# Attention: a chunk's value sum turned by TensorE transposes into unused score columns, its parts added by GpSimd

## The reference

```python
qkv = x @ w_attn
...
att = jnp.einsum('bhtd,bhsd->bhts', q, k) * (1.0 / math.sqrt(hd))
causal = jnp.tril(jnp.ones((T, T), dtype=bool))
att = jnp.where(causal, att, -jnp.inf)
att = jax.nn.softmax(att, axis=-1)
...
att = att.reshape(B, H, 2, T, T)
att = att[:, :, 0] - lambda_full * att[:, :, 1]
out = jnp.einsum('bhts,bhsd->bhtd', att, v)
```

## Time and profile before

| | us |
|---|---|
| median of 3 executions | 3572.49 (3572.16 to 3578.31) |
| the profiled execution | 3580.86 |
| its span | 3579.1 |
| PE busy in it | 3336.4 (93%) |
| DVE busy | 2745.6 (77%) |
| ACT busy | 2214.7 (62%) |
| POOL busy | 1518.2 (42%) |

### The profile page before, as it was taken

One profiled execution on the slowest core, in us unless ns is written; L12 is line 12 of the kernel. 1 busy time (PEld: TensorE's weight loads), 2 busy tenths in 40 slices (PEclk: granted clock), 3 DMA queues, 4 the chain that ended last, 5 costly groups with the idle time before them and its releaser, 6 DMA issues. The chain is left out here.

```text
span 3579.1 us, 59642 instructions
## 1 busy us (share of the span) xinstructions
PE 3336.4 (93%) x19650; PEld 1381.1 (39%) x19663; DVE 2745.6 (77%) x4938; ACT 2214.7 (62%) x3459; POOL 1518.2 (42%) x1881
## 2 busy tenths in 40 slices
PE   8998999999999999999999999866999999999997
PEld 5564666643333333333333333252333333333332
DVE  4654223568898888898898889384899989899898
ACT  3331221137777777777777777745777767777763
POOL 2225000013333332323333333313887888887886
PEclk9999999989999999999999999987999999999999
DMA  4443111111111111110111110041222222222221
GB/s 154 132 156 110 45 44 44 42 35 40 49 38 31 35 37 34 33 32 26 29 34 34 34 31 25 11 136 53 61 82 75 69 80 74 69 80 75 66 75 53
DMA packets 160886, 211.60 MB, mean 59 GB/s; under 512 B 32324, under 2 KB 108364, under 8 KB 160604
## 3 DMA queue, kind: packets, MB, share of 16 engines
q1 hardware_dynamic: 141340, 172.51, 16.3%
q0 software_dynamic: 8512, 18.76, 1.7%
q10 hardware_dynamic: 10752, 16.78, 1.4%
HBM read 154.48 MB, written 52.69 MB: 58 GB/s over the span
## 5 line engine op out<-in xcount | busy, mean ns | idle before, releaser
L1270 ACT ACTIVATE prob<-psS 128x1024 f32<-128x1024 f32 (+3 forms) x1280 | 1100.2, 905 | 332.0 <-PE psS L1437 326.1
L1329 DVE TENSOR_REDUCE pmax<-psR 128x1 f32<-128x512 f32 x1674 | 1060.8, 684 | 139.2 <-PE psR L1384 100.1
L1384 PE MATMUL psR<-kslab,qslab 48*128 48x512 bf16 (+3 forms) x2480 | 675.2, 353 | 55.6 <-DVE pmax L1329 23.0
L2100 POOL TENSOR_TENSOR hc<-h_d,crep 128x512 f32<-128x512 f32 x512 | 647.2, 1272 | 184.2 <-DVE h_d L2318 135.9
L1437 PE MATMUL psS<-qslab,kslab 51*128 51x512 bf16 (+3 forms) x2560 | 638.0, 351 | 5.1 <-ACT prob L1270 4.4
L1452 PE MATMUL psVo<-prob,vaug 128*32 128x512 f32 (+3 forms) x5120 | 625.2, 544 | 0.9 <-ACT ov L1274 0.9
L1202 POOL TENSOR_SCALAR_AFFINE_SELECT prob<-prob 128x256 f32<-128x256 f32 (+1 forms) x512 | 209.3, 421 | 774.0 <-ACT prob L1270 773.7
L2318 DVE TENSOR_TENSOR_SCAN h_d<-a,state,psU 128x512 f32<-128x512 f32 x384 | 489.4, 1275 | 0.0
L1384 PEld LDWEIGHTS psR<-kslab,qslab 48*128 48x128 bf16 x2480 | 181.7, 94 | 789.7 <-DVE pmax L1329 462.1
L2308 DVE TENSOR_TENSOR psU<-dtx,psX 128x512 f32<-128x512 f32 x512 | 355.9, 695 | 119.5 <-PE psX L2471 44.3
L2225 ACT ACTIVATE a<-dt,a_neg 128x512 f32<-128x512 f32 x512 | 366.2, 723 | 57.8 <-DVE h_d L2318 56.5
(11 more groups left out here) (297 smaller groups left out, 4854.4 us busy)
## 6 DMA issues: line engine op xcount, KB each, us to landing
crep<-c_rows_d SPq DMA_DIRECT2D x256, 256.0 KB, 3.2
x_e<-rows_d SPq DMA_DIRECT2D x72, 128.0 KB, 2.0
y_d<-y SPq DMA_DIRECT2D x72, 128.0 KB, 1.7
q_d<-parts SPq DMA_DIRECT2D x48, 128.0 KB, 2.4
k_d<-parts SPq DMA_DIRECT2D x48, 128.0 KB, 4.1
qslab<-q_d SPq DMA_DIRECT2D x60, 96.0 KB
kslab<-k_d SPq DMA_DIRECT2D x60, 96.0 KB
x<-in_L_attn_x_dram SPq DMA_DIRECT2D x8, 512.0 KB, 5.9
```

Of the source, the lines that this page charges most:

```text
L1270: act.activation(prob[g % BUFS][:, :, off:BLK], psS[g % 2][:, :, off:BLK], ACT.Exp).then_inc(prob_ready, 1)
L1329: dve.tensor_reduce(into[:, lo:lo + (count - 1) * NEXT + 1:NEXT], psR[at % BANKS][:, 0:count * w].rearrange("p (n w) -> p n w", w=w), AX.X ...
L1384: ins = pe.matmul(dst[:, m * w:(m + 1) * w], qslab[u][rows, i * P:(i + 1) * P], kslab[u][rows, ch * BLK:ch * BLK + w], start=(m == 0), sto ...
L2100: pool.tensor_tensor(hc[:, g % CR], h[:, g % HR], crep[:, g // PAIR % SPR], ALU.mult).then_inc(hc_ready, 1)
```

## The change

Per chunk, `fold_sum` no longer takes a bank of `psR`. It turns the four blocks of `ov` with float32 transposes (`ident` as the moving operand, 128 columns each) into columns 0 to 255 of both banks of `psS[g % 2]`, on a diagonal step whose scores use columns 256 on only. The four folds stand at steps 11, 22, 38 and 50 (step 10 of the next head), after the step's lead item and ahead of its scores. ScalarE copies them after the step's exponentials, 4 x 4 x 17 columns, and the scores of step g+2 wait for that copy too. `o_head` now holds the even and the odd part apart. GpSimd adds them (`add_sums`, step 12 of the next head), VectorE takes the reciprocal there (step 14), and GpSimd multiplies by lambda and combines (step 16). The constant `fold` and what made it in the stage before go. The ring `psR` holds only max items and the turned maxima.

```diff
-        FOLD = LAG + 3
-        POST = FOLD + 3
...
+        FOLD_AT = [LAST[1], LAST[1] + TPB * 3 - 1, LAST[3] - 1, NSTEP + LAST[1] - 1]
+        for c, k in enumerate(FOLD_AT):
+            assert k > LAST[c] + LAG and STEPS[k % NSTEP][2] >= 2 * P
+        SUM_AT, WEIGHTS_AT, POST_AT = FOLD_AT[-1] + 2, FOLD_AT[-1] + 4, FOLD_AT[-1] + 6
+        END = TOTAL - NSTEP + POST_AT + 1
+        VALUES_AT = LAG + 3
...
-        o = sb("o_head", [P, 2, ST_T, 2, OC])
+        o = sb("o_head", [P, 2, ST_T, 2, 2, OC])
+        osum = sb("o_sum", [P, ST_T, 2, OC])
...
+            def add_sums(n):
+                pool.wait_ge(fold_copied, BPB * n + BPB + CREDIT)
+                pool.wait_ge(post, 5 * n + CREDIT)
+                pool.tensor_tensor(osum[:], o[:, n % 2, :, :, 0], o[:, n % 2, :, :, 1], ALU.add).then_inc(post, 1)
+
             def combine(n):
                 pool.wait_ge(rs_ready, n + 1 + CREDIT)
...
+                pool.wait_ge(post, 5 * n + 1 + CREDIT)
+                pool.tensor_tensor(rl[:], rs[:, :, 1], lam[:, 1:2].to_broadcast([P, ST_T]), ALU.mult).then_inc(post, 1)
...
-            def copy_fold(n, c):
-                at = PLACE[("fold", n, c)]
-                act.wait_ge(ring_full, at + 1 + CREDIT)
+            def copy_fold(g, n, c):
+                act.wait_ge(scores_done, min(g, TOTAL) + 1 + CREDIT)
                 if n >= 2:
-                    act.wait_ge(post_done, n - 1 + CREDIT)
-                act.copy(o[:, n % 2, TPB * c:TPB * c + TPB].rearrange("p i a d -> p (i a d)"),
-                         psR[at % BANKS][:, 0:TPB * 2 * OC]).then_inc(ring_free[at % BANKS], 1)
+                    act.wait_ge(post, 5 * (n - 1) + CREDIT)
+                act.copy(o[:, n % 2, TPB * c:TPB * c + TPB].rearrange("p (x y) a s d -> p x (y a s) d", x=2),
+                         psS[g % 2][:, :, 0:2 * P].rearrange("p x (y d) -> p x y d", d=VW)[:, :, :, 0:OC])\
+                   .then_inc(fold_copied, 1)
...
             def weights(n):
-                freed(dve, ("fold", n, BPB - 1))
-                dve.wait_ge(post_done, n + CREDIT)
-                dve.reciprocal(rs[:], o[:, n % 2, :, :, VD]).then_inc(rs_chain, 1)
-                dve.wait_ge(rs_chain, n + 1 + CREDIT)
-                dve.tensor_scalar(rl[:], rs[:, :, 1], lam[:, 1:2], None, ALU.mult).then_inc(rs_ready, 1)
+                dve.wait_ge(post, 5 * n + 1 + CREDIT)
+                dve.reciprocal(rs[:], osum[:, :, :, VD]).then_inc(rs_ready, 1)
...
+            def scores_free(g):
+
+                pe.wait_ge(prob_ready, min(g - 1, TOTAL) + CREDIT)
+                for m, c in folds_at(g - 2):
+                    pe.wait_ge(fold_copied, FOLDS.index((m, c)) + 1 + CREDIT)
+
+            def fold_sum(g, n, c):
+                scores_free(g)
                 pe.wait_ge(ov_ready, BPB * n + c + 1 + CREDIT)
-                dst = take(("fold", n, c))
                 for i in range(TPB):
-                    ins = pe.matmul(dst[:, i * 2 * OC:(i + 1) * 2 * OC], ov[c % 2][:, i * P:(i + 1) * P],
-                                    fold[:].rearrange("p a d -> p (a d)"), start=True, stop=True)
-                ins.then_inc(ring_full, 1)
+                    ins = pe.transpose(psS[g % 2][:, i // 2, i % 2 * P:i % 2 * P + P], ov[c % 2][:, i * P:(i + 1) * P],
+                                       keep["ident"][:])
+                if g >= TOTAL:
+                    ins.then_inc(scores_done, 1)
...
                 if lead:
                     max_products(lead[1], lead[2])
                     got = got[1:]
+                for n, c in folds_at(g):
+                    fold_sum(g, n, c)
                 if g < TOTAL:
                     scores(g, (1, 0) if lead and ITEMS[lead[2]][0] == 0 else (0, 1))
```

More of the change, by code:

```diff
@@ L651, in phase_experts @@
         kslabs, qslabs = keep["kslabs"], keep["qslabs"]
-        ident_b, mask_q, fold, lam_in, lam_s = (keep[x] for x in ("ident_b", "mask_q", "fold", "lam_in", "lam_s"))
+        ident_b, mask_q, lam_in, lam_s = (keep[x] for x in ("ident_b", "mask_q", "lam_in", "lam_s"))
         lam_w = sb("lam_w", [P, 2, HD])
@@ L780, in _ @@
             c.after(pool.memset(mask_q[:], 0.0))
-            c.after(pool.memset(fold[:], 0.0))
             c.after(pool.memset(keep["bias_d"][:], 0.0))
@@ L800, in _ @@
             c.wait()
-            for odd in range(2):
-                c.after(pool.affine_select(out=fold[:], in_=fold[:], compare_op=ALU.not_equal, fill=1.0,
-                                           base=-VW * odd, pattern=[[-2 * VW, 2], [-1, OC]], channel_multiplier=1))
         @block.scalar
@@ L978, in phase_attention @@
         LAG = 4
-        FOLD = LAG + 3
-        POST = FOLD + 3
         TURN = 2
         AHEAD = 0.26
-        END = TOTAL + POST + 1
         LAST = [max(k for k, s in enumerate(STEPS) if s[0] == c) for c in range(BPB)]
         DIAG = [k for k, (c, st, off, first) in enumerate(STEPS) if st >= TPB * c]
+        FOLD_AT = [LAST[1], LAST[1] + TPB * 3 - 1, LAST[3] - 1, NSTEP + LAST[1] - 1]
[4 more added lines that the diff above has]
+        VALUES_AT = LAG + 3
         MIX = 3
@@ L995, in phase_attention @@
         SLABS = 2
-        ident_b, mask_q, fold, lam_s = (keep[x] for x in ("ident_b", "mask_q", "fold", "lam_s"))
+        ident_b, mask_q, lam_s = (keep[x] for x in ("ident_b", "mask_q", "lam_s"))
         pmax = keep["pmax"]
@@ L1039, in phase_attention @@
         mpart_ready = sem("b_mpart_ready")
-        rs_chain = sem("b_rs_chain")
+        fold_copied = sem("b_fold_copied")
         rs_ready = sem("b_rs_ready")
-        pchain = sem("b_pchain")
+        post = sem("b_post")
         v_ready = sem("b_v_ready")
-        post_done = sem("b_post_done")
         mix_in = [sem(f"b_mix_in{s}") for s in range(MIX)]
@@ L1087, in fills_at, with folds_at @@
                 got.append(("turn", n + 1, 0))
[L1088 to L1091, removed]
-            return got
+            return got
+        def folds_at(g):
+            return [(m, c) for m in (g // NSTEP - 1, g // NSTEP) for c in range(BPB)
+                    if 0 <= m < NH and NSTEP * m + FOLD_AT[c] == g]
+        FOLDS = [fold for g in range(END) for fold in folds_at(g)]
         FILLS = [fills_at(g) for g in range(END)]
@@ L1203, in mask @@
                                    pattern=[[0, 2], [1, w]], channel_multiplier=-1).then_inc(prob_masked, 1)
+            def add_sums(n):
+                pool.wait_ge(fold_copied, BPB * n + BPB + CREDIT)
+                pool.wait_ge(post, 5 * n + CREDIT)
+                pool.tensor_tensor(osum[:], o[:, n % 2, :, :, 0], o[:, n % 2, :, :, 1], ALU.add).then_inc(post, 1)
             def combine(n):
                 pool.wait_ge(rs_ready, n + 1 + CREDIT)
[L1207 to L1213, removed]
+                pool.wait_ge(post, 5 * n + 1 + CREDIT)
+                pool.tensor_tensor(rl[:], rs[:, :, 1], lam[:, 1:2].to_broadcast([P, ST_T]), ALU.mult).then_inc(post, 1)
+                pool.tensor_tensor(o1[:], osum[:, :, 0, 0:VD], rs[:, :, 0:1].to_broadcast([P, ST_T, VD]), ALU.mult)\
+                    .then_inc(post, 1)
+                pool.wait_ge(post, 5 * n + 3 + CREDIT)
+                pool.tensor_tensor(o2[:], osum[:, :, 1, 0:VD], rl[:].unsqueeze(2).to_broadcast([P, ST_T, VD]),
+                                   ALU.mult).then_inc(post, 1)
+                pool.wait_ge(post, 5 * n + 4 + CREDIT)
+                pool.tensor_tensor(o_rows[:, n], o1[:], o2[:], ALU.subtract).then_inc(post, 1)
             def gather(n):
@@ L1247, in _ @@
                     mask(n, k)
-                if 1 <= n < NH - 1 and k == FOLD:
+                if 1 <= n < NH - 1 and k == VALUES_AT:
                     values(n + 1)
@@ L1255, in _ @@
                     cut_max(n + 1)
-                for m, c in sums_at(g, POST):
-                    if c == BPB - 1:
-                        combine(m)
+                if 0 <= g - SUM_AT and (g - SUM_AT) % NSTEP == 0:
+                    add_sums((g - SUM_AT) // NSTEP)
+                if 0 <= g - POST_AT and (g - POST_AT) % NSTEP == 0:
+                    combine((g - POST_AT) // NSTEP)
         @block.scalar
@@ L1293, in _ @@
                     exponentials(g)
+                for n, c in folds_at(g):
+                    copy_fold(g, n, c)
                 for kind, n, c in FILLS[g]:
-                    if kind == "fold":
-                        copy_fold(n, c)
                     if kind == "turn":
@@ L1359, in _ @@
                 fills(FILLS[g])
-                for n, c in sums_at(g, POST):
-                    if c == BPB - 1:
-                        weights(n)
+                if 0 <= g - WEIGHTS_AT and (g - WEIGHTS_AT) % NSTEP == 0:
+                    weights((g - WEIGHTS_AT) // NSTEP)
         @block.tensor
@@ L1421, in fills @@
                         max_mask(n, x)
-                    elif kind == "fold":
-                        fold_sum(n, x)
                     else:
@@ L1433, in scores @@
                 if g >= 2:
```

(3 more changed lines are left out.)

1 line of the change is left out of this document (removed).

## The result

The changed kernel takes 3584.61 us (median; 3582.72 to 3586.6), the kernel before on the same chip 3578.99 us. The ratio is 1.0018, with a 95% interval of 1.001 to 1.0027: 0.18% slower, where 0.14% was forecast. In us the two can only be compared as differences, +5.6 measured against +5 forecast: the forecast of 3577.5 us stood on a median of three executions, 3572.49 us, and over ten executions the kernel before takes 3578.99. The profiled execution's span is 3584.9 us, 5.8 more than before.

What follows compares the result with a forecast made beforehand. Neither TensorE nor VectorE bounds throughout; each waits for the other. Walking head 12 gave about 0.18 us more a head, over 29 heads about +5 us: 3585.9 profiled, less 8.4 for the median, 3577.5 us; range 3562 to 3592.

Steps and rivals of the forecast that it cites:

- The price of a block: Time one new fold's transposes put between lead item and scores on TensorE: 0.31 + 0.33 + 0.21 = 0.85 us.
- Points 2, 5 and 7 of the walk: New folds in head 12: two for one at steps 10, 11 cost 0.18 us; step 22, 0.69; step 38, 0.85.
- lost pairing: Before the transposes the lead item no longer runs beside scores; this loss was counted inside its 0.31 us.
- Point 1: Fold of step 6 gone: only VectorE's dry wait before the reduce at 1366.53 comes back, gain 0.56 us.
- Point 3: Reciprocal moved to step 14, into a VectorE backlog: costs 0.26 us, leaving a running gain of 0.12 us.
- Points 4 and 6: Folds of steps 18 and 30 gone: the waiting TensorE work gets its ring bank 0.63 us sooner each time.
- ScalarE's copy, GpSimd's addition, the masks: Copy of 0.39 us, addition of about 1.1 us at step 12, masks moved ahead of combining: all taken as hidden.
- Dearer blocks: Slower rival: each 0.1 us more per new fold at steps 10, 11, 22, 38 gives 3589 us; chance 0.31.
- The larger relief: Faster rival: VectorE has more slack or the reciprocal fits a wait; a head 0.28 us shorter, 3564 us; chance 0.18.
- TensorE's time did not count everywhere: Denies the rival that all 128 folds save four passes each in full, 56 us, giving 3516 us; chance 0.03.
- Transposes in two passes or end to end: Rival: 0.27 us per transpose in place of 0.11, 75 us more, giving 3653 us; chance 0.03.
- The ends: First head gains about 0.3 us; last gains about 0.6, its addition costs 1.1 less 0.5; nothing taken for both.

## Why the prediction came out right, point by point

- **Bound and method.** That saved TensorE time counts only where VectorE is dry, and that the new folds stand in just those places, is what the runs showed: the eight-pass folds at the new steps paid their full 4 x 0.42 us, the transposes at the old steps kept 1.15 us a head of the 1.6 that they saved on TensorE.
- **The price of a block** was 0.06 us too low, 0.91 instead of 0.85. This is the term of the sum that was mis-sized. It is the three transposes at 0.11: the second starts 0.17 us behind the first. The earlier trace rows show transposes behind a product of the same tile shape; the first of a block comes behind another, which goes with the delay but is not shown to be its cause. Points 2, 5 and 7 of the walk came out dearer by 0.09, 0.08 and 0.04 us.
- **The reason given for it** was wrong. I put the lead item's 0.31 us down to a lost pairing with the scores. With the transposes behind the scores the pairing is back and a block costs the same at step 38. Only the size of the term was right (0.32 us measured).
- **Point 1** was 0.08 us too careful: the reduce starts beside the reading of the accumulator (1367.91) and not behind it.
- **Point 3**, the reciprocal in the backlog, was right in kind and 0.07 us too dear. The run that moved it gave the 0.19 us back.
- **Points 4 and 6**, where the ring place decides: +0.62 and +0.57 against +0.63 twice.
- **ScalarE's copy, GpSimd's addition, the masks:** hidden in the walk, as said. The addition shows only behind the last scores of the stage.
- **The rivals.** Dearer blocks came true by half the size that I gave them. The larger relief came true in two small parts (0.08 us at point 1, 0.07 at point 3) that the blocks outweighed. TensorE's time did not count everywhere: it is busy less and the head is longer. Transposes in two passes or end to end did not come (512 products, 0.11 us apart behind the first two). One of them is 287 ns long on average, and four take 0.66 us. The 275 ns that the Trainium skill gives ("TensorE: Matmul & The Clock Gate", Part 4) agree with that length, which is not the price of one among several.
- **The ends** were a sum of errors that cancel. From the first scores to the last combining the stage is 9.9 us longer, not 5: 29 heads make 10.4 (8.6 by 0.30 a head, 1.1 by a stretch at the lower clock in one head, 0.7 by small delays in others), the first and the last two give back 1.5, and the path behind the last scores is 1.0 longer. Ahead of it the kernel is 1.2 us shorter, and behind it 3.0. The first scores of the other versions come between 774.4 and 776.7 us (778.9 with the eight passes at the new steps), so the 1.2 may be chance. Behind it all ten experiments are 3.0 to 6.2 us shorter than the kernel before, of which there is one trace, so whether these 3.0 us belong to the change stays open. The forecast of 0.14% against 0.18% measured is therefore closer than the working was, by luck: of the stage alone I had half (5 of 9.9 us).

## What to carry to other kernels

Where two engines hand work to each other through a short ring, find for each place which one is behind before pricing an edit there; a cheaper form of an operation can lose to its new place. Here the form was worth 35 us and the place took it all; taken apart, the form with better places made 39 us and more. Count the places in a ring as well as the engines' time, and put small instructions of an engine into its waits: one step beside a wait the reciprocal cost 0.16 us of its 0.35.

## What had not been expected of the hardware

- A first transpose of a block, behind a product of another tile shape, delays the second by 0.06 us more than in the earlier trace rows (four fill 0.66 us against 0.60). In the ring, behind two wide products side by side, it is 0.03 (0.63 us at 1365.83 above). The change of shape is not needed for it: in the trace of the kernel before six transposes at 2388.33 us, behind a product of their own shape and 0.83 us of idleness, fill 0.87 us, where those of the earlier trace rows would fill 0.82. What causes it stays open.
- With eight passes per fold at the diagonal steps TensorE was granted 1.2 GHz for a stretch in 19 of 31 head distances, 1.12 us each; with four transposes there in one (1.14 us), with eight passes at the old steps in none. The work ahead of the falls was as dense in the run without them (TensorE busy 47.83 of 50.40 us here, 46.27 of 48.46 in the earlier trace rows). What decides it stays open.
